# Transposing the probabilities on VectorE in every tile, with later layernorm units in the middle blocks

## The reference

```python
q = (src @ Wq + bq).reshape(B, nb, 64, 8, 128)      # k, v alike; src = layernorm(x)
scores = einsum('bnqhd,bnkhd->bhnqk', q, k) * 128 ** -0.5
out = einsum('bhnqk,bnkhd->bnqhd', softmax(scores), v).reshape(B, S, D)
x = x + out @ Wo + bo
h = square(relu(layernorm(x) @ W_fc.T))             # 4096 wide
x = x + spikes(h @ W_proj.T) / 5                    # 0 to 5, by thresholds on y
```

## Time and profile before

| | us |
|---|---|
| median of 3 runs | 707.44 (707.12 to 707.58) |
| profiled execution | 707.24 |
| its span, slowest core | 705.6 |
| spans of the eight cores | 702.7 to 705.6 |

### The profile page before, as it was taken

One profiled execution on the slowest core, in us unless ns is written; L12 is line 12 of the kernel. 1 busy time (PEld: TensorE's weight loads), 2 busy tenths in 40 slices (PEclk: granted clock), 3 DMA queues, 4 the chain that ended last, 5 costly groups with the idle time before them and its releaser, 6 DMA issues.

```text
span 705.6 us, 10623 instructions; the slowest of 8 cores (702.7 to 705.6 us)
## 1 busy us (share of the span) xinstructions
PE 691.9 (98%) x3772; PEld 323.3 (46%) x3772; DVE 390.9 (55%) x589; ACT 179.7 (25%) x330; POOL 49.7 (7%) x96
## 2 busy tenths in 40 slices
PE   7999999999999999999999999999999999999996
PEld 3544444444444444444444444444444444444444
DVE  5327863776687488337655227845225865221476
ACT  3544550460351135130003331002331002332000
POOL 2211110211005000000000000000000000000000
PEclk9999999999999999999999999999999999999998
DMA  8998996598669995496461002272002152000011
GB/s 182 210 152 148 160 163 185 117 218 202 157 180 204 247 209 93 145 168 182 122 177 60 1 1 61 67 202 89 1 1 61 37 142 88 32 0 2 30 46 46
DMA packets 31012, 80.94 MB, mean 115 GB/s; under 512 B 5616, under 2 KB 5872, under 8 KB 30192
## 3 DMA queue, kind: packets, MB, share of 16 engines
q0 software_dynamic: 12960, 31.46, 26.0%
q1 hardware_dynamic: 15552, 40.39, 20.3%
q10 hardware_dynamic: 2448, 8.40, 3.0%
HBM read 82.33 MB, written 16.78 MB: 140 GB/s over the span
## 4 chain that ended last, share of the span: by engine, by line
PE 93%; DMA 4%; DVE 1%; issue 1%; POOL 0%; DVEq 0%; POOLq 0%
PE ps_m L439 31%; PE ps_y L517 30%; PE ps_m L386 13%; PE ps_m L412 8%; PE ps_m L426 8%; DMA wq_sb<-Wq 4%; DVE acc_sb L785 1%; PE ps_y L466 1%; PE ps_y L499 1%; PE ps_m L524 0%; PE ps_t L478 0%; DVE acc_sb L782 0%; DVE xr L790 0%; PE ps_t L368 0%; POOL wq_sb L879 0%
## 5 line engine op out<-in xcount | busy, mean ns | idle before, releaser
L439 PE MATMUL ps_m<-xn2t,w_sb 128*128 128x512 bf16 x1024 | 222.3, 379 | 0.0
L517 PE MATMUL ps_y<-w_sb,h_sb 128*128 128x512 bf16 (+1 forms) x1024 | 218.3, 376 | 0.0
L439 PEld LDWEIGHTS ps_m<-xn2t,w_sb 128*128 128x128 bf16 x1024 | 99.9, 98 | 120.1
L517 PEld LDWEIGHTS ps_y<-w_sb,h_sb 128*128 128x128 bf16 x1024 | 100.2, 98 | 117.6
L606 ACT ACTIVATE h_sb<-ps_m 128x512 bf16<-128x512 f32 x128 | 76.3, 597 | 263.4 <-PE ps_m L439 263.4
L775 DVE TENSOR_TENSOR h_sb<-h_sb 128x512 bf16<-128x512 bf16 x128 | 53.0, 424 | 121.5 <-ACT h_sb L606 121.3
L785 DVE SCALAR_TENSOR_TENSOR acc_sb<-ps_y,acc_sb 128x1024 bf16<-128x1024 f32 (+2 forms) x72 | 78.6, 1092 | 7.5
L386 PE MATMUL ps_m<-xnt,wq_sb 128*128 128x512 bf16 x240 | 56.8, 379 | 2.4 <-DMA wq_sb<-Wq 2.2
L386 PE MATMUL ps_m<-xnt,wk_sb 128*128 128x512 bf16 x248 | 58.6, 379 | 0.4 <-DMA wk_sb<-Wk 0.4
L412 PE MATMUL ps_m<-wv_sb,xnt 128*128 128x512 bf16 x256 | 56.6, 379 | 0.0
L426 PE MATMUL ps_m<-wo_sb,attn_sb 128*128 128x512 bf16 x256 | 55.9, 379 | 0.0
(11 more groups left out here) (66 smaller groups left out, 364.9 us busy)
## 6 DMA issues: line engine op xcount, KB each, us to landing
xr<-x SPq DMA_DIRECT2D x32, 512.0 KB, 7.3
xl<-x SPq DMA_DIRECT2D x96, 128.0 KB, 3.9
w_sb<-Wfc POOLq DMA_DIRECT2D x32, 256.0 KB, 9.8
x<-xr ACTq DMA_DIRECT2D x16, 512.0 KB, 5.2
out<-xr POOLq DMA_DIRECT2D x12, 512.0 KB, 2.9
w_sb<-Wpr POOLq DMA_DIRECT2D x16, 256.0 KB, 33.4
xn2t<-blk SPq DMA_DIRECT2D x64, 64.0 KB, 2.0
w_sb<-Wpr POOLq DMA_DIRECT2D x4, 1024.0 KB, 15.6
```

The lines of the kernel that those rows point to most:

```text
L439: m = E.matmul(bank(key)[:], w1_sb[fc // 4][:, k0:k0 + 128], tokens(xn2t, c, 0, 4), start=(c == 0), stop=(c == 7))
L517: return E.matmul(out, h_sb[fc][:, tt * 128:(tt + 1) * 128], w2_sb[fc // 4][:, k0:k0 + n], start=(fc == 0), stop=(fc == 31))
```

## The change

VectorE transposes the probabilities of all four tiles. turn_p, p_copy and the two ways of placing scores are gone; every block uses p_turn, in slots 2, 6, 10 and 13 (14 in block 0), with one buffer p_sb and four buffers pt_sb. The values matmuls stand in slots 15 and 18 of blocks 1 to 3. The v copies of blocks 1 and 2 go from DVE to ACT. In blocks 1 and 2 the layernorm units begin in slots 3, 12, 16 and 20. The programs of SP and POOL are as before.

```diff
 def turn_p_pair(b, s):
-    slots = [2, 6, 10, 14 if b == 0 else 13] if b in BY_BLOCKS else [5, 9, 14, 17]
+    slots = [2, 6, 10, 14 if b == 0 else 13]
 def values_four(b, s):
-    slots = [16, 24] if b == 0 else [14 if b in BY_BLOCKS else 13, 18]
+    slots = [16, 24] if b == 0 else [15, 18]
+LN_FIRST = {-1: (3, 6, 9, 12), 0: (13, 17, 21, 25), 1: (3, 12, 16, 20), 2: (3, 12, 16, 20)}
 def ln_unit(b, s, step):
-    first, apart = {-1: (3, 3), 0: (13, 4)}.get(b, (3, 4))
-    n, rest = divmod(s - first - step, apart)
-    return 4 * (b + 2) + n if b <= 2 and rest == 0 and 0 <= n < 4 else None
+    firsts = LN_FIRST.get(b, ())
+    return 4 * (b + 2) + firsts.index(s - step) if s - step in firsts else None
@@ tensor_program
-        def turn_p(p, j):
-            E.wait_ge(ve_p, 4 * p + j + 1)
-            turn_free(("pt", p, j))
-            for i in range(4):
-                m = E.transpose(ps_t[:, i * 128:(i + 1) * 128],
-                                p_buffer(p, j)[:, i * 128:(i + 1) * 128], ident[:])
-            m.then_inc(full_t, 1)
         def values(p, f):
-            E.wait_ge(*p_turned(p, 2 * f + 1))
+            E.wait_ge(ve_pt, 4 * p + 2 * f + 2)
@@ scalar_program
-                if b < 1 or key[0] != "v":
-                    main(key)
+                main(key)
@@ vector_program
         def softmax_scale(p, j):
-            if p in BY_BLOCKS and j > 0:
-                E.wait_ge(*p_turned(p, j - 1))
-            if p == 1 and j == 1:
-                E.wait_ge(full_v, 4)
+            if p + j > 0:
+                E.wait_ge(ve_pt, 4 * p + j)
         def p_turn(p, j):
             if p > 0:
-                E.wait_ge(full_v, 4 * p)
+                E.wait_ge(full_v, 4 * p - 2 + 2 * (j // 2))
-        def p_copy(p, j):
-            E.wait_ge(full_t, turn_no[("pt", p, j)] + 1)
-            E.tensor_copy(pt_buffer(p, j)[:], ps_t[:, 0:512]).then_inc(free_t, 1)
                 if (j := turn_p_pair(b, s)) is not None:
-                    if b in BY_BLOCKS:
-                        p_turn(b, j)
-                    else:
-                        p_copy(b, j)
+                    p_turn(b, j)
-                if b > 0 and key[0] == "v":
-                    v_copy(key)
```

More of the change, by code:

```diff
@@ L76, in block_keys @@
     return [("up", 0, fc) for fc in range(EARLY_UP)]
-BY_BLOCKS = (0, 3)
 def scores_four(b, s):
@@ L160, in turn_order @@
                 keys.append(("x", i))
-            if b not in BY_BLOCKS and (j := turn_p_pair(b, s)) is not None:
-                keys.append(("pt", b, j))
     return {k: n for n, k in enumerate(keys)}
@@ L201, in build_nc @@
     attn_sb = at("attn_sb", ATTN_AT, 4096, BF16)
-    p_sb = [at(f"p_sb_{i}", WORK + 57344 + 1024 * i, 512, BF16) for i in range(2)]
-    pt_sb = [at(f"pt_sb_{i}", WORK + a, 512, BF16) for i, a in enumerate([59392, 60416, 58368, 96256])]
+    p_sb = at("p_sb", WORK + 57344, 512, BF16)
+    pt_sb = [at(f"pt_sb_{i}", WORK + a, 512, BF16) for i, a in enumerate([58368, 59392, 60416, 96256])]
     bo_sb = at("bo_sb", WORK + 61440, 1024, F32)
@@ L292, in emptied @@
         return free_m[main_no[key] % 3], main_no[key] // 3 + 1
[L294 to L309, removed]
     def values_bank(h):
@@ L462, in scores @@
                 E.wait_ge(*emptied(("k", p, h)))
-                for bl in sorted(range(8), key=lambda bl: scores_at(p, bl)):
-                    half, col = scores_at(p, bl)
-                    s0 = (h % 4) * 256 + col * 64
+                for bl in (0, 2, 4, 6, 1, 3, 5, 7):
+                    q0 = (bl % 2) * 64
+                    s0 = (h % 4) * 256 + (bl // 2) * 64
                     m = E.matmul(
-                        ps_s[half * 64:half * 64 + 64, s0:s0 + 64],
+                        ps_s[q0:q0 + 64, s0:s0 + 64],
                         q_sb[:, h * 512 + bl * 64:h * 512 + (bl + 1) * 64],
@@ L490, in values @@
                     kb = (bl % 2) * 64
-                    pt = pt_buffer(p, h // 2)[kb:kb + 64, :]
-                    if p in BY_BLOCKS:
-                        probs = pt.rearrange("p (b g t) -> p g b t", b=2, g=8)[:, (h % 2) * 4 + bl // 2, :, :]
-                    else:
-                        p0 = (h % 2) * 256 + (bl % 4) // 2 * 128 + (bl // 4) * 64
-                        probs = pt[:, p0:p0 + 64]
+                    g = (h % 2) * 4 + bl // 2
+                    pt = pt_sb[h // 2][:].rearrange("p (b g t) -> p g b t", b=2, g=8)
                     o0 = (bl % 2) * 512 + (h % 2) * 256 + (bl // 2) * 64
@@ L499, in values @@
                     m = E.matmul(values_bank(h)[:, o0:o0 + 64], v_sb[kb:kb + 64, v0:v0 + 128],
-                                 probs, start=True, stop=True)
+                                 pt[kb:kb + 64, g, :, :], start=True, stop=True)
                 if h % 2 == 1:
@@ L538, in tensor_program @@
                     turn_x(i)
-                if b not in BY_BLOCKS and (j := turn_p_pair(b, s)) is not None:
-                    turn_p(b, j)
                 if (f := scores_four(b, s)) is not None:
@@ L722, in softmax_scale @@
             E.wait_ge(ve_c, c)
-            if p in BY_BLOCKS and j > 0:
-                E.wait_ge(*p_turned(p, j - 1))
-            if p == 1 and j == 1:
-                E.wait_ge(full_v, 4)
-            E.tensor_tensor(p_buffer(p, j)[:].rearrange("p (g k) -> p g k", g=8), e8,
+            if p + j > 0:
+                E.wait_ge(ve_pt, 4 * p + j)
+            E.tensor_tensor(p_sb[:].rearrange("p (g k) -> p g k", g=8), e8,
                             rsum[:].unsqueeze(2).broadcast_to([128, 8, 64]),
@@ L732, in p_turn @@
         def p_turn(p, j):
-            blocks = p_buffer(p, j)[:].rearrange("p (g b t) -> p g b t", g=8, b=2)
-            turned = pt_buffer(p, j)[:].rearrange("p (b g t) -> p g b t", b=2, g=8)
+            blocks = p_sb[:].rearrange("p (g b t) -> p g b t", g=8, b=2)
+            turned = pt_sb[j][:].rearrange("p (b g t) -> p g b t", b=2, g=8)
             if p > 0:
-                E.wait_ge(full_v, 4 * p)
+                E.wait_ge(full_v, 4 * p - 2 + 2 * (j // 2))
             E.wait_ge(ve_p, 4 * p + j + 1)
```

## The result

The changed kernel takes **742.16 us** (median of 4 runs, 740.27 to 743.95) against 707.51 for the kernel before beside it: ratio 1.0487, 95% interval 1.0473 to 1.0501, 34.7 us slower. The forecast was 735, the range 714 to 750.

The account below looks back on a forecast made before the run. PE, busy 98% of the span, was taken to bound the kernel. 707.24 - 1.76 (transposes) + 9.9 (block 1) + 17 (block 2) + 3.5 (clock) = 735.9, rounded down to 735 us; range 714 to 750.

Parts of the forecast that it names:

- PE's gain of 1.76 us: Blocks 1 and 2: removing PE's 32 transposes saves 0.88 us in each, all on the path.
- DVE's list up to scale(13): Block 1: DVE's work through the second layernorm unit's scale takes 32.7 us, ending at 155.1, 14.4 us later than before.
- Who waits for scale(13): Block 1, SP's in-order queue: xl 15, xr and tile 3's loads wait; xr begins at 158.4, blocks(15) ends at 175.6.
- Where PE waits in block 1: PE waits 6.2 us at the fourth o group, then for turned tile 3; block 1 costs 9.9 us together.
- Block 2: Same lateness, with SP's loads sharing DMA engines with POOL's weights: tile 4 turned 15.5 to 21 us late.
- the chosen 17 us: Block 2: cost of the late turned tile 4 at up(0,0), picked from 15.5 to 21 us.
- The clock: TensorE after PE's four waits: each may cost 0 or 1.7 us; two taken, 3.5 us, at most 6.9.
- The sum: Whole kernel: profiled 707.24 us less the transposes, plus both blocks and the clock, gives 735.9, rounded to 735.
- The rival "faster": Whole kernel: transposes' 1.76 us come out and no wait replaces them, 705.5 us; chance 0.06.
- The half microsecond of cover for the values: Slot 18: DVE's last p_turn ends 31.9 us after the first reduce, slot 18 begins at 32.5; up to 1 us per block.

Follow-up runs that it names:

- all_mended: Changed kernel with four xl buffers, turned tiles 3 and 4 issued by SP and ACT, W2's first four loads and W1's sixth after tile 4: 706.85 us, ratio 0.9984.
- before_mended: Kernel before with four xl buffers, turned tiles issued by SP and ACT, and W2's first loads after tile 4 is turned: 708.65 us, ratio 1.0009.
- w2_late: Changed kernel with 16 of block 2's 24 weight pieces issued by POOL only after tile 4 is turned: 729.61 us, ratio 1.0298.
- filled_waits: Changed kernel with 12 and 44 unneeded matmuls ahead of PE's waits for turned tiles 3 and 4: 739.89 us, ratio 1.0442.
- turns_only: Changed kernel with the layernorm units of blocks 1 and 2 back in slots 3, 7, 11 and 15: 719.16 us, ratio 1.0169.

## Why the prediction was right, point by point

Where a time is said to be on the forecast's clock, 0.9 us are added to it, as the profiled core began block 1 so much sooner than the one on which the forecast was built.

- **PE's gain of 1.76 us** was right within 0.4: 1.4 us in the traces of all_mended and before_mended, 1.8 (0.6 to 2.9) in their run times.
- **DVE's list up to scale(13)**, summed from block 3: 155.1 forecast, 155.0 measured on the forecast's clock. xr issued at 158.4 forecast, 158.3 measured.
- **Who waits for scale(13)**: the chain held, with blocks(15) at 175.6 forecast and 175.5 measured. What the working lacked is xl(15), the first load behind the same wait. "DVE reaches add_bo in slot 20 well before that" was true by 1.0 us only: DVE waited 5.95 us for xl first and 1.6 for xr after it. As xr landed last, leaving xl out cost the forecast nothing here; that is luck, and the experiments show it. Letting xr go first brings back 6 us, freeing both brings back 22.
- **Where PE waits in block 1**: 6.2 us at the fourth o group was forecast; it was 3.50 at the first, by ACT's v copies behind a late ln_rstd(15), and 0.89 at the fourth. That ln_rstd, late because of xl(15), was named as a risk and priced at nothing. The wait for tile 3 was 4.3 (3.7 forecast). Since its DMAs set when q(3,0) begins, the total held all the same: 10.7 us late on the forecast's clock, 9.9 forecast.
- **Block 2**: the reason given, SP's loads sharing the DMA engines with POOL's, is borne out by w2_late. The xr loads came as forecast: the third at 245.8 (245 forecast), the fourth at 248.8 (250), blocks(19) at 248.3 (247.4). The term that was mis-sized most is the turning of tile 4. It took 24.1 us from the first issue to the last landing, where the working had 16.8 from the kernel before and, if all must follow the fourth xr, 22.6 at most. up(0,0) began 24.5 us after blocks(19), where the chosen 17 us had 18.6. The first reduce of block 2 was also placed wrongly: the scores stand ahead of q(3,0) and need not wait for tile 3, so it came at 186.2 and not 190.6, and then DVE waited 7.8 us for exp, which stands behind the copy of q(3,0) on ACT.
- **The clock** was mis-sized too: two dips of 1.7 us, 3.5 in all, were forecast, with 6.9 as the most. PE lost 10.3 us at the lower clock, in five stretches of 1.7 to 2.8. Waits of 3 to 4 us brought a dip as well, and a dip cost up to 2.8, where the start, from which 1.7 was taken, had less.
- **The sum**: PE's waits are 26.6 us and 26.9 were forecast, so that the clock looks like the whole of the missing 7 us between 735 and 742. That agreement is luck. The slow work ahead of up(0,0) made PE some 6 us late there, and the turned tile came 6.8 us later than forecast, so the waits between them stayed the same. Along the chain that decides, up(0,0) began at 272.8 where 266.0 was forecast: 5.9 us of it by the turning of tile 4 and 0.9 by a later blocks(19). What follows took 2.3 us longer than before, where 3.5 was set down for the clock. The rest is the rounding from 735.9 to 735 and the difference between the profiled execution and the median. filled_waits agrees: time came back behind up(0,0), and hardly ahead of it.
- **The rival "faster"** needed blocks(15) by 166.0 and blocks(19) by 222. In the changed kernel they ended at 174.6 and 248.3. In all_mended, brought to the clock of the kernel before, they end at 167.7 and 226.4, so even with no load late the limits are missed by 1.7 and 4.4 us; PE doesn't wait because tile 3 is turned in about 8 us and tile 4 in 7, where it was 14.7 and 16.8. The forecast had named just this as what would be needed.
- **The half microsecond of cover for the values** was never tested by the change; turns_only shows how thin it is, through exp and ACT's copies rather than through p_turn.

## What to carry to other kernels

When work on an off-path engine is moved later, follow its waiters into the in-order DMA queue: every load behind the one that waits is late as well, and the price is paid where those loads are used. Taking away one of two parallel causes brings back little (here 6 of 35 us); so look at which one is first in the queue, and remove the common wait (here with a third and fourth buffer). When PE idles, count the wait and the slow work behind it: here 26.6 us of waits were followed by 10.3 us lost at the lower clock. But slow work ahead of a wait that a DMA ends costs little, so add up along the chain that decides, and not over all waits. And take a transfer's time from a stretch in which the other queues are as full as they will be then.

## What the runs showed of the hardware that was not expected

- TensorE's clock after a wait: 3.5 us of idleness was followed by a granted clock of 0.78 over 7.9 us, 10.8 us by 0.84 over 17.2; the five stretches behind waits, of 3 to 11 us, cost 1.7 to 2.8 us of work each, so a short wait cost about as much of it as a long one. Matmuls without use in the wait kept it at 1.00.
- The landing of the same 64 KB transfers from SP's queue: 12.0 to 14.5 us for the last ones of tile 4 in the changed kernel, 2.0 to 3.1 in w2_late, with the same number issued at about the same pace. The two kernels differ only in when POOL issues 16 weight pieces, so what waits in another queue sets it.
- Two queues instead of one brought 16 DMAs home in 13.5 us instead of 25.6 while a third queue was full; why the landing itself became shorter was not separated.
